# A graph layer on one core: five rounds a period in place of eight, three PSUM count buffers in place of two

## The reference, cut to what matters

```python
h = jnp.maximum(_layernorm(x, axis=-1), 0.0)
msg = h[src] + edge_attr                              # (206250, 64)
agg = jax.ops.segment_sum(msg, dst, num_segments=6250)
hid = jax.nn.relu(agg @ W1 + b1)                      # (6250, 128)
out = x + hid @ W2 + b2
```

## Time and profile before

| | us |
|---|---|
| median of 3 runs | 531.18 |
| lowest, highest | 528.41, 531.21 |
| the profiled execution | 530.76 |
| its span on the core | 529.1 |
| TensorE busy | 470.9 (89%) |
| VectorE busy | 432.1 (82%) |
| ScalarE busy | 352.9 (67%) |
| GpSimd busy | 283.3 (54%) |

### The profile page before, as it was taken

One profiled execution on the slowest core, in us unless ns is written; L12 is line 12 of the kernel. 1 busy time (PEld: TensorE's weight loads), 2 busy tenths in 40 slices (PEclk: granted clock), 3 DMA queues, 4 the chain that ended last, 5 costly groups with the idle time before them and its releaser, 6 DMA issues.

```text
span 529.1 us, 27474 instructions
## 1 busy us (share of the span) xinstructions
PE 470.9 (89%) x12541; PEld 417.4 (79%) x12541; DVE 432.1 (82%) x481; ACT 352.9 (67%) x503; POOL 283.3 (54%) x223
## 2 busy tenths in 40 slices
PE   1013799899999999999999999999999999998996
PEld 1002698789888989888888988988898898887885
DVE  4989997888888888888789788889889889858650
ACT  3837676676776677767767767767777777775720
POOL 4489993565275465547547547555754754216000
PEclk9999999999999999999999999999999999998999
DMA  9657139636455364553644635546464454633300
GB/s 203 178 151 226 46 112 233 192 109 191 114 146 162 110 177 127 141 166 106 172 139 118 189 111 148 155 125 183 107 179 131 140 168 111 188 97 106 93 7 9
DMA packets 139623, 73.62 MB, mean 139 GB/s; under 512 B 23644, under 2 KB 137550, under 8 KB 139382
## 3 DMA queue, kind: packets, MB, share of 16 engines
q1 hardware_dynamic: 136105, 65.30, 44.8%
q0 software_dynamic: 3168, 4.90, 2.9%
q10 hardware_dynamic: 234, 1.65, 1.0%
HBM read 66.98 MB, written 4.86 MB: 136 GB/s over the span
## 4 chain that ended last, share of the span: by engine, by line
PE 87%; DVE 5%; DMA 3%; issue 2%; ACT 2%; POOL 0%; SPq 0%; ACTq 0%; DVEq 0%
PE sum_ps L821 27%; PE sum_ps L843 19%; PE count_ps L808 19%; PE sum_ps L829 14%; PE head_ps L858 3%; PE head_ps L865 3%; DVE lo_hot L654 2%; DMA comb_rows<-counts 1%; PE turn_ps L793 1%; DVE hi_hot L654 1%; DMA dst_sb<-in_dst 1%; ACT counts L324 1%; DMA ell<-comb_rows,ell_idx 1%; ACT counts L326 1%; DVE h_parts L620 1%
## 5 line engine op out<-in xcount | busy, mean ns | idle before, releaser
L386 ACT CAST counts<-count_ps 128x784 bf16<-128x784 f32 x391 | 298.6, 817 | 98.3 <-PE count_ps L808 98.3
L654 DVE TENSOR_TENSOR lo_hot<-iota_lo,codes 128x4096 bf16<-128x4096 bf16 x98 | 224.4, 2290 | 43.5 <-ACT codes L353 31.7
L821 PE MATMUL sum_ps<-counts,h_parts 128*128 128x256 bf16 (+1 forms) x1225 | 151.2, 273 | 3.5 <-issue 3.5
L488 POOL DMA_INDIRECT ell<-comb_rows,ell_idx x50 | 76.8, 1536 | 135.5 <-DVE ell_idx L626 101.2
L808 PE MATMUL count_ps<-hi_hot,lo_hot 64*128 64x49 bf16 x6256 | 123.7, 183 | 17.4 <-DVE hi_hot L654 12.9
L808 PEld LDWEIGHTS count_ps<-hi_hot,lo_hot 64*128 64x128 bf16 x6256 | 100.6, 94 | 40.0 <-DVE hi_hot L654 13.8
L821 PEld LDWEIGHTS sum_ps<-counts,h_parts 128*128 128x128 bf16 x1225 | 112.2, 98 | 23.6 <-issue 5.1
L468 POOL DMA_INDIRECT g<-in_dst,row_i x49 | 99.5, 2031 | 55.4 <-DVE e_hot L668 39.9
L843 PE MATMUL sum_ps<-e_hot,edges 128*64 128x24 f32 x3528 | 118.2, 214 | 0.0
L843 PEld LDWEIGHTS sum_ps<-e_hot,edges 128*64 128x64 f32 x3528 | 118.2, 138 | 0.0
L654 DVE TENSOR_TENSOR hi_hot<-iota_hi,codes 128x1600 bf16<-128x1600 bf16 x98 | 101.1, 1032 | 0.0
(11 more groups left out here) (107 smaller groups left out, 221.9 us busy)
## 6 DMA issues: line engine op xcount, KB each, us to landing
edges<-in_edge_attr SPq DMA_DIRECT2D x98, 576.0 KB, 5.6
h_rows<-h_sb SPq DMA_DIRECT2D x1, 1568.0 KB, 9.7
x_sb<-in_x SPq DMA_DIRECT2D x4, 384.0 KB, 10.2
out<-o_sb SPq DMA_DIRECT2D x24, 64.0 KB, 3.7
comb_rows<-counts ACTq DMA_DIRECT2D x1, 1443.8 KB
dst_rows<-in_dst SPq DMA_DIRECT2D x49, 18.0 KB
ell<-comb_rows,ell_idx POOLq DMA_INDIRECT x50, 4.7
g<-in_dst,row_i POOLq DMA_INDIRECT x49, 5.9
```

Of the source, the lines that this page charges most:

```text
L386: nc.scalar.copy(counts[j % 2][:, :, 0:2 * half].rearrange("p s (h i) -> p h s i", h=2)[:, :, :, 8 * u:8 * u + 8], count_ps[g % 2][:, :, 0 ...
L488: nc.gpsimd.indirect_dma_start(out=ell[j % 2][0:rows, h, :, :].rearrange("p s w -> p (s w)"), out_offset=None, in_=comb_dram[:, :], in_off ...
L654: return nc.vector.tensor_tensor(out_ap.rearrange("p i (a t) -> p i a t", t=2), bc(table_ap.rearrange("p (o a t) -> p o a t", o=1, t=2), [ ...
L821: nc.tensor.matmul(sum_ps[m % 2][:, 0:cols], parts[:, s, 0:2 * F], counts[m % 2][:, s, 0:cols], start=(s == 0), stop=False, skip_group_che ...
```

## The change

- A period has five rounds. Each has three count steps of eight or nine pairs, and the batches of VectorE's tables are 26, 26, 26, 25 and 25 pairs (19, 19 and 18 in the last period), one batch a round.
- There are three buffers `count_ps`; a count step waits for the copy of the step three before. They take six banks, and the two banks of the head and the transposes are given up.
- `hidden`, `rows`, the transposes, the row sums at the start and the few matmuls at the end write into that one of the two `sum_ps` banks in which no sums are being made. For this the transposes wait for `rows_added`, the high sums of round 0 wait also for `rel_copied` and `codes_made`, and the last ones for a new semaphore `far_read`.
- High sums: 20, 0, 20, 0 and 9 in the five rounds (tables `HIGH`, `LOW` of first indices); low sums: 0, 5, 0, 12 and 32. Edge sums of a whole tile in rounds 1 and 3, ahead of the low ones. Both transposes at the end of round 2, the shift matmul in round 3, the transpose of `worst` in round 2 of the last period.
- On VectorE `match` moves from batch 1 to 2, `add_rows` from batch 1 to 3, the copy of the shifted index from batch 3 to 4. On ScalarE the ReLU moves behind step 2, both transposed results are taken behind step 8.

```diff
-    BATCH = 32
+    BATCH = 26
+    ROUNDS, STEPS = 5, 15
...
+    BATCHES = [[26, 26, 26, 25, 25], [19, 19, 18]]
...
-        count_ps = [ps(f"count_ps{b}", [P, 2, 512]) for b in range(2)]
+        count_ps = [ps(f"count_ps{b}", [P, 2, 512]) for b in range(3)]
...
-        head_ps = ps("head_ps", [P, 512])
...
+        def hid_ps(f):
+            return sum_ps[f % 2][:, 0:2 * P]
...
+        def codes_ps(j):
+            return sum_ps[(j + 1) % 2][:, 3 * P:4 * P].bitcast(bf16)
...
-                        if b == 1 and j + 1 < DTS:
+                        if b == 2 and j + 1 < DTS:
                             match(j + 1)
-                        if b == 1 and j >= 2:
+                        if b == min(3, batches_of(j) - 1) and j >= 2:
                             add_rows(j - 2)
...
                     if j >= 1:
                         pe.wait_ge(codes_made, j)
-                        pe.wait_ge(rel_copied, j)
+                    if j >= 3:
+                        pe.wait_ge(rows_added, j - 2)
...
-                    if u % 4 == 0:
+                    if u % 3 == 0:
                         pe.wait_ge(hots_made, n + 1)
-                    if g >= 2:
-                        pe.wait_ge(copied, g - 1)
+                    if g >= 3:
+                        pe.wait_ge(copied, g - 2)
...
+                HIGH = [0, 20, 20, 40, 40, 49]
+                LOW = [0, 0, 5, 5, 17, 49]
...
+                            high_sums(m, range(HIGH[v], HIGH[v + 1]))
+                            if v % 2 == 1 and v // 2 < tiles_in(m):
+                                edge_sums(m, v // 2, range(TILES_E))
+                            if LOW[v] < LOW[v + 1]:
+                                last = low_sums(m, range(LOW[v], LOW[v + 1]))
...
-                        if v == 3 and j < DTS:
+                        if v == 2 and j + 1 < DTS:
+                            turn_codes(j + 1)
+                        if v == 2 and j < DTS:
                             turn_rel(j)
-                        if v == 4 and j + 1 < DTS:
-                            turn_codes(j + 1)
-                        if j == LAST - 2 and v == 6:
+                        if j == LAST - 2 and v == 3:
```

## The result

The changed kernel takes 521.66 us (median; 520.01 to 522.73), the kernel before in the same comparison 530.67. The ratio is 0.983, 95% interval 0.981 to 0.986: **faster by 1.7%, where the forecast was 0.6% slower** and the range was 524 to 542. The profiled execution took 520.01 us, its span is 518.3.

The account below looks back on a forecast made before the run. TensorE was taken as the bound, its period going from 18.70 to 18.95 us. Span 529.1 - 0.2 + 5.3 + 0.25 - 2.5 + 0.6 = 532.55, plus 1.66 outside the span: 534.2 us, range 524 to 542.

Parts of the forecast that it names:

- what 0.21 us is: TensorE's idle time ahead of counts: the array emptying at a change of shape, not a wait for a copy.
- The formula: TensorE run ending in another tile shape: 0.135 us plus its columns' streaming time at 2.4 GHz (256 columns 0.1067 us).
- 2.40 for the edge sums of a tile: TensorE, rounds 1 and 3: edge sums of a whole tile priced at 2 x 1.18 + 0.04 = 2.40 us.
- +0.68 for low sums that now empty the array: TensorE, per period: low sums cost 3.07 us in place of 2.39, since all three runs empty the array.
- Forecast +0.25 a period: TensorE's five rounds sum to 18.95 us against 18.70 before; +5.3 us over periods 2 to 22.
- Rival B: TensorE outruns its instruction supply: gaps all gone 526.8 us (chance 0.12), or twice as many 541.6 us (0.12).
- Period 23: Period of 22.49 us, 3.8 over 18.70: forecast to change by -2.5 us, and +0.25 for the pace.
- the 1.06: Period 23: 1.06 us that the counts' loads wait for VectorE, forecast to go.
- The 1.24: Period 23: 1.24 us in which TensorE's loads wait for nothing shown; whether it stays was left open.
- 0.17 shorter: ScalarE copies the same 12,544 columns in 15 steps in place of 16: some 0.17 us less.
- "removes nothing": Third count buffer and ScalarE's fewer copy steps: no gain on the path, as ScalarE was not late in 18.70 us.
- Forecast -0.2 and +0.6: Start: VectorE's shorter batches, -0.2 us; end: low sums exposed in period 24, +0.5, and the last period, +0.1.

Follow-up runs that it names:

- second trace of the changed kernel: The changed kernel run again with nothing altered, beside the kernel before: 521.21 us, ratio 0.982.
- Thin loads: 64 KB in place of 576 KB in each load of edge features from the fifth tile on: kernel before 522.61 us, changed kernel 520.35 us.
- the first kernel with loads held apart: Changed kernel with all low sums beside edge sums, three of a period's four edge-feature loads now waiting for count steps: 520.04 us, ratio 0.978.

## Why the prediction was wrong

**The bound, and what 0.21 us is.** Right. TensorE sets the pace, the 0.21 is the array emptying at a change of shape, and the third buffer removes none of it in eight rounds (531.11 against 531.32). The formula held for all runs of sums in the changed kernel: 5 low sums 0.45 (0.455), 12 0.79 (0.775), 9 high sums 1.09 (1.095), 32 low sums 1.87 (1.84), 20 high sums with hidden ahead within 0.02. The rule in the Trainium skill (TensorEngine Tiling, Key Properties), that a change of tiling mode drains the engine, agrees; its size comes from the rows alone. One reading of the prediction goes too far: that no load is pulled ahead at a change of shape. At 385.37 two loads of counts stand ahead of the last 36x128 load; the 0.26 for the turn of the rel rows, taken from the old order, holds it already.

**The failed term: 2.40 for the edge sums of a tile.** They take 2.10 (379.64 to 381.74, 29 ns a load). I took 1.18 for 36 loads from rows in which low sums stood ahead of them, and had noted myself that their backlog hides under the edge loads. Hidden is not free: the 1.22 held it. Then I charged the same backlog a second time, as +0.68 for low sums that now empty the array. Priced together, low and edge sums of a half tile cost 1.79 in the old order and 1.83 in the other. So 0.30 too much in each of two rounds. The count rounds, 0.77 in place of 0.805 for 52 and 0.74 in place of 0.775 for 50, are 0.17 less in all, and small excesses in the others take back 0.07. Forecast +0.25 a period, measured -0.45: 0.70 x 21 = 14.7 us, more than the whole miss of 12.5.

**Gaps without a releaser.** Rival B's mechanism was right: TensorE ran through its instructions faster than they came. I had nothing to size it with and kept it out of the sum; the excess over the clean pace in periods 2 to 22, mostly these gaps, fell from 6.2 to 2.3 us, -3.9. In the second trace of the changed kernel it is 5.1, of which 3.7 in the first period alone; in the 20 periods behind that one it is 1.6 and 1.4 against 5.0 of the kernel before. Thin loads show that the loads of edge features bring them about: with thin ones the kernel before has 0.9 us of excess in 21 periods in place of 6.2. The changed order does not ask for instructions more slowly; with its low sums moved to the edge sums it lost 15 us to them by the traces (393.99 against 379.03) and 12 by the medians. That it had few was not to be read from the trace of before.

**Period 23.** Forecast 20.2 (22.49 - 2.25), measured 18.64. That the 1.06 goes was right. The 1.24, which I left open, stands at a mark and is gone with thin loads even in the old order (19.64).

**VectorE, ScalarE, the buffers.** Right that they are off the path: no wait for the add, VectorE 16.18 (16.6). ScalarE did not get 0.17 shorter; it is busy 14.65 in 18.24 where the old order has 13.57 in 18.70, with room for it. A copy of the same shape got slower, and not by the buffers: 817 ns before, 818 with three buffers in eight rounds, 935 with three and 933 with two in five rounds. Why was not tested. In the changed kernel, by its groups:

```profile
L409 ACT CAST counts<-count_ps 128x882 bf16<-128x882 f32 x192 | 188.1, 1024 | 57.5 <-PE count_ps L833 56.4
L409 ACT CAST counts<-count_ps 128x784 bf16<-128x784 f32 x168 | 149.5, 935 | 0.0
```

But "removes nothing" was half an answer: with two buffers the five rounds cost 5.6 us a period more.

**Start and end.** Forecast -0.2 and +0.6; measured +3.63 at the first copy and, up to the last copy, -0.31. In the second trace of the changed kernel the first copy is only 1.2 late, but with the period behind it it is 3.3; the first trace has 2.7. The move of `match` past VectorE's second batch was costed at nothing; it makes a gather take 12.37 us, for which VectorE waits 2.6 at 67 us. Why that gather is so slow is open: DMA is busy 22% then, and VectorE runs without a pause in the old order too. The sum had no term for the clock. The second trace has the full clock up to the first copy, and there the copy is 1.2 late; so some 2.4 of the 3.63 go with the stretch at half clock. The +3.1 at the end belongs to neither order: the kernel before with 64 idle transposes has it as well, and it is TensorE's last branch, 3.6 us in place of 0.47.

## What to carry to other kernels

A time taken from start to start behind another run holds that run's backlog: take prices only from rows whose predecessor you keep, or price the pair. An effect named as hidden has to stand somewhere in the sum, once. And where a gap has no releaser, number the engine's instructions: if the gaps stand at multiples of a fixed count, the fetch is a suspect. The packets' times in the DMA queue show whether they come late, and thinning or spreading the other DMA traffic shows whether that delays them, as it did here.

## What was not expected of the hardware

- TensorE stops at 256-instruction marks (16 KB) when its packet is late, up to 2.8 us a time here (at 90.25 us in the first kernel with loads held apart). With thin loads the packet started 0.8 us after the mark before on average, with full ones 1.4 to 1.9; ahead of the gaps of the kernel before it started 2.4 to 4.3 after it. TensorE resumed 1.2 to 1.6 after its end.
- The branch at the end of the program took TensorE 0.47 us in three layouts and 3.4 to 4.1 in the others, with a 16 KB instruction packet coming in between.
- One chip ran the same kernel 3.5% slower (549 against 530), with gaps of 0.5 us in runs of fp32 edge loads; with edge sums first they are often 10 or 12 instructions apart. Their cause is open.
- An order that is 0.22 us a period better in its work (18.03 against 18.25) was 6 us slower in all (527.63 against 521.21), since it met late instructions more often: 21 gaps in 21 periods against two or three.
